# V for all heads ahead of the attention, tile 0 of the output projection scaled in the last head, and projection and gate_up in one block

## What is computed

```python
mod = silu(c) @ w_mod                      # six rows of 512: sa, ca, ga, sb, cb, gb
ga, gb = sign(g) * maximum(abs(g), 0.25)   # of both gates
h = layernorm(x) * (1 + ca) + sa
k, q, v = einsum(W_K, h), einsum(W_Q, h), einsum(W_V, h)       # per head
scores = q . k, below the diagonal (tril), others -1e10
attn = softmax(scores / sqrt(128));  z = attn @ v
x = x + ga * einsum('df,bqf->bqd', W_O, z_flat)
h = layernorm(x) * (1 + cb) + sb
gate, up = h @ dequant_fp4(gate_up)        # codes of 4 bits, scales per 128 inputs
y = (silu(gate) * up) @ dequant_fp4(down)
x = x + gb * y / sqrt(mean(y * y) + 1e-6)
```

## Time and profile before

| | us |
|---|---|
| median of the runs | 2183.33 |
| profiled execution | 2183.67 |
| its span, first to last instruction | 2181.7 |
| prologue | 0 to 57.4 |
| attention | 57.4 to 1664.7 |
| output projection | to 1877 |
| gate_up and down | to 2181.7 |

### The profile page before, as it was taken

One profiled execution on the slowest core, in us unless ns is written; L12 is line 12 of the kernel. 1 busy time (PEld: TensorE's weight loads), 2 busy tenths in 40 slices (PEclk: granted clock), 3 DMA queues, 4 the chain that ended last, 5 costly groups with the idle time before them and its releaser, 6 DMA issues. The chain is left out here.

```text
span 2181.7 us, 37262 instructions
## 1 busy us (share of the span) xinstructions
PE 2112.4 (97%) x12305; PEld 1845.1 (85%) x12305; DVE 1353.7 (62%) x3062; ACT 1059.6 (49%) x2006; POOL 719.3 (33%) x546
## 2 busy tenths in 40 slices
PE   6899999999999999999999999999997999899899
PEld 3698989898889989898988989898986788788687
DVE  7465655656565656556565646455564587699865
ACT  4354545455454545445454545455453333588511
POOL 3333343334243343443350101000017344388300
PEclk9999999999999999999999999999998999999999
DMA  5111110110111010111100000000006576111121
GB/s 207 40 41 35 35 34 32 35 43 22 46 46 34 34 34 31 34 34 34 46 25 26 25 12 24 12 22 15 25 21 192 175 245 221 57 40 39 46 70 63
DMA packets 84004, 122.79 MB, mean 56 GB/s; under 512 B 9315, under 2 KB 49891, under 8 KB 83939
## 3 DMA queue, kind: packets, MB, share of 16 engines
q1 hardware_dynamic: 81635, 117.76, 16.6%
q10 hardware_dynamic: 2304, 4.20, 0.5%
HBM read 87.97 MB, written 33.95 MB: 56 GB/s over the span
## 5 line engine op out<-in xcount | busy, mean ns | idle before, releaser
L978 DVE TENSOR_TENSOR pT_lo<-ps_t,pT_hi 128x512 fp32r<-128x512 f32 (+3 forms) x640 | 360.3, 605 | 219.9 <-ACT pT_hi L895 219.7
L903 ACT ACTIVATE probs<-probs,rmin 128x128 f32<-128x128 f32 (+15 forms) x256 | 307.9, 1203 | 225.7 <-DVE rmin L969 224.7
L895 ACT ACTIVATE pT_hi<-ps_t 128x512 fp32r<-128x512 f32 (+3 forms) x640 | 304.9, 534 | 87.5 <-PE ps_t L831 86.2
L197 PE MATMUL ps_z<-pT_hi,v_hi 128*128 128x256 f32 (+1 forms) x1152 | 326.4, 283 | 0.0
L198 PE MATMUL ps_z<-pT_lo,v_hi 128*128 128x256 f32 (+1 forms) x1152 | 325.4, 282 | 0.0
L199 PE MATMUL ps_z<-pT_hi,v_lo 128*128 128x256 f32 (+1 forms) x1152 | 324.8, 282 | 0.0
L197 PE MATMUL ps_p<-hT_hi,w_hi 128*128 128x512 f32 x768 | 309.6, 403 | 8.6 <-PEq L277 4.1
L199 PE MATMUL ps_p<-hT_hi,w_lo 128*128 128x512 f32 x768 | 301.9, 393 | 0.0
L198 PE MATMUL ps_p<-hT_lo,w_hi 128*128 128x512 f32 x768 | 301.2, 392 | 0.0
L831 PE MATMUL ps_t<-ident,probs 128*128 128x128 f32 x2176 | 278.9, 274 | 3.1 <-DVE pT_lo L978 1.6
L831 PEld LDWEIGHTS ps_t<-ident,probs 128*128 128x128 f32 x2176 | 247.3, 141 | 19.1 <-DVE pT_lo L978 2.1
(11 more groups left out here) (140 smaller groups left out, 3861.2 us busy)
## 6 DMA issues: line engine op xcount, KB each, us to landing
scratch_zT<-z SPq DMA_DIRECT2D x256, 64.0 KB, 1.6
o_z<-scratch_zT SPq DMA_DIRECT2D x31, 512.0 KB, 7.0
o_scales<-scratch_recips SPq DMA_DIRECT2D x31, 512.0 KB, 7.8
w_raw<-in_w_qkv SPq DMA_DIRECT2D x16, 768.0 KB, 4.6
p_wmod<-in_w_mod SPq DMA_DIRECT2D x6, 1024.0 KB, 10.6
words<-in_gu_packed SPq DMA_DIRECT2D x44, 128.0 KB, 3.5
scratch_wgu<-deq_a SPq DMA_DIRECT2D x22, 256.0 KB, 2.0
g_codes<-scratch_wgu SPq DMA_DIRECT2D x11, 512.0 KB, 3.4
```

The source lines that it names most:

```text
L197: nc.tensor.matmul(dst, stat[0], mov[0], start=start, stop=False)
L895: nc.scalar.activation(pT[0][:, slot, i % 2, 0:w], ps_t[:, (chunks_before(i) + u) % T_BANKS, 0:w], ACT.Copy).then_inc(t_hi, 1)
L903: nc.scalar.activation(probs[:, i % 2, 0:w], probs[:, i % 2, 0:w], ACT.Exp, bias=rmin[:, i % 2:i % 2 + 1], scale=-1.0, accum_out=sums[:, i ...
L978: nc.vector.tensor_tensor(pT[1][:, slot, i % 2, 0:w], ps_t[:, (chunks_before(i) + u) % T_BANKS, 0:w], pT[0][:, slot, i % 2, 0:w].bitcast(F ...
```

## The change

- **V pass.** The prologue computes V for all 16 heads, in 64 tiles of 128 tokens by four heads, with the tokens' hT as stationary operand, so that V needs no transposes. GpSimd (for the first group of heads, ScalarE with it) splits the V weights; ScalarE and VectorE split each tile of V, and SP saves both parts to a scratch tensor "v" in HBM, in two buffers. The prologue's steps are now in written orders too.
- **Attention.** The V and V^T units are gone, with their weights; SP loads both parts of V per head in four blocks of 512 tokens (load_v), the first two at the head's start. All three orders are new. Words, code, deq_a and deq_b lie in a buffer that belongs to tile 0 of the projection.
- **Last head.** SP loads z and reciprocals of tile 0, GpSimd scales all but head 15's part after the fourth part of W_O.
- **Output projection and gate_up** are one block: the projection returns its programs, and gate_up runs them first. The last tile's transposing and modulation stand among the first steps of gate_up. The gate scales are turned at tile 5 instead of 1. The first loads for down are issued behind the third load of gate codes.

The diff, cut to its core (in head of SP, attention):

```diff
 PE_ORDER = """
-    S0.0 S1.0 Z7.1- PW0 T0.0 T1.0 Z7.2- PK1.0 PK1.1 PK1.2 PK1.3 Z7.3- S2.0 N0- PQ1.0 PQ1.1 PQ1.2 PQ1.3 S3.0 Z0.0 T2.0
-    S4.0 S4.1 PV1.0 PV1.1 PV1.2 PV1.3 T3.0 T4.0 T4.1 S5.0 S5.1 PW1 Z1.0 S6.0 S6.1 S7.0 PK2.0 PK2.1 PK2.2 PK2.3 T5.0
-    T5.1 T6.0 S7.1 PQ2.0 PQ2.1 PQ2.2 PQ2.3 Z2.0 Z2.1 PV2.0 PV2.1 PV2.2 PV2.3 T6.1 T7.0 T7.1 PW2 S8.0 S8.1 S8.2 Z3.0
-    PK3.0 S9.0 S9.1 S9.2 PK3.1 Z3.1 PK3.2 PK3.3 T8.0 T8.1 T8.2 S10.0 S10.1 PQ3.0 PQ3.1 PQ3.2 PQ3.3 S10.2 T9.0 T9.1
-    T9.2 S11.0 S11.1 S11.2 Z4.0 T10.0 T10.1 T10.2 Z4.1 Z4.2 PV3.0 PV3.1 PV3.2 PV3.3 S12.0 S12.1 S12.2 S12.3 PW3 T11.0
-    T11.1 T11.2 S13.0 S13.1 S13.2 S13.3 Z5.0 T12.0 T12.1 Z5.1 Z5.2 T12.2 T12.3 T13.0 S14.0 S14.1 S14.2 PQ0.0+ PQ0.1+
-    S14.3 PQ0.2+ PQ0.3+ T13.1 T13.2 T13.3 S15.0 S15.1 S15.2 S15.3 Z6.0 Z6.1 Z6.2 T14.0 T14.1 T14.2 Z6.3 PK0.0+ PK0.1+
-    T14.3 T15.0 T15.1 PK0.2+ PK0.3+ T15.2 T15.3 Z7.0 PV0.0+ PV0.1+ PV0.2+ PV0.3+
+    S0.0 S1.0 S2.0 T15.0- T15.1- T15.2- PQ1.0 PQ1.1 PQ1.2 PQ1.3 Z7.0- Z7.1- T15.3- Z7.2- S3.0 Z7.3- N0- T0.0 T1.0
+    PK2.0 PK2.1 PK2.2 PK2.3 T2.0 S4.0 Z0.0 S4.1 PQ2.0 PQ2.1 PQ2.2 PQ2.3 T3.0 T4.0 T4.1 S5.0 S5.1 S6.0 Z1.0 PK3.0 S6.1
+    S7.0 S7.1 T5.0 T5.1 PK3.1 S8.0 S8.1 Z2.0 Z2.1 T6.0 T6.1 T7.0 S8.2 PK3.2 S9.0 T7.1 PK3.3 Z3.0 Z3.1 S9.1 S9.2 T8.0
+    T8.1 T8.2 S10.0 S10.1 PQ3.0 PQ3.1 PQ3.2 PQ3.3 S10.2 T9.0 T9.1 T9.2 S11.0 S11.1 S11.2 Z4.0 Z4.1 Z4.2 T10.0 T10.1
+    T10.2 S12.0 S12.1 S12.2 T11.0 T11.1 T11.2 PQ0.0+ S12.3 PQ0.1+ S13.0 Z5.0 Z5.1 Z5.2 S13.1 S13.2 S13.3 T12.0 T12.1
+    T12.2 S14.0 S14.1 T12.3 S14.2 PQ0.2+ PQ0.3+ S14.3 T13.0 T13.1 T13.2 S15.0 S15.1 PK0.0+ PK0.1+ PK0.2+ PK0.3+ Z6.0
+    Z6.1 T13.3 T14.0 T14.1 Z6.2 Z6.3 S15.2 S15.3 T14.2 T14.3 PK1.0+ PK1.1+ PK1.2+ PK1.3+
 """
...
 DVE_ORDER = """
-    C0.0 C1.0 X0 UW0 L0.0 L1.0 UK1 C2.0 UQ1 C3.0 L2.0 C4.0 C4.1 L3.0 L4.0 L4.1 C5.0 C5.1 UW1 C6.0 C6.1 X1 UK2 L5.0
-    L5.1 L6.0 C7.0 C7.1 UQ2 L6.1 L7.0 UW2 L7.1 C8.0 C8.1 C8.2 C9.0 C9.1 C9.2 X2 UK3 L8.0 L8.1 L8.2 C10.0 C10.1 C10.2
-    UQ3 L9.0 C11.0 C11.1 L9.1 L9.2 C11.2 L10.0 L10.1 L10.2 C12.0 C12.1 C12.2 C12.3 UW3 L11.0 C13.0 C13.1 C13.2 L11.1
-    L11.2 C13.3 L12.0 L12.1 L12.2 L12.3 L13.0 C14.0 C14.1 C14.2 C14.3 C15.0 L13.1 L13.2 L13.3 C15.1 C15.2 C15.3 UQ0+
-    R0 L14.0 L14.1 L14.2 L14.3 L15.0 L15.1 UK0+ L15.2 L15.3
+    C0.0 UK1 L15.0- L15.1- L15.2- UQ1 C1.0 L15.3- C2.0 X0 L0.0 L1.0 C3.0 UK2 L2.0 C4.0 C4.1 UQ2 L3.0 L4.0 L4.1 C5.0
+    C5.1 C6.0 X1 C6.1 C7.0 L5.0 L5.1 C7.1 C8.0 L6.0 L6.1 L7.0 C8.1 L7.1 C8.2 C9.0 X2 C9.1 C9.2 UK3 L8.0 L8.1 L8.2
+    C10.0 C10.1 C10.2 UQ3 L9.0 L9.1 L9.2 C11.0 C11.1 C11.2 L10.0 L10.1 L10.2 C12.0 C12.1 L11.0 L11.1 L11.2 C12.2 C12.3
+    C13.0 C13.1 C13.2 C13.3 L12.0 L12.1 L12.2 C14.0 C14.1 L12.3 C14.2 C14.3 UQ0+ L13.0 L13.1 L13.2 UK0+ C15.0 L13.3
+    L14.0 L14.1 C15.1 C15.2 C15.3 L14.2 L14.3 R0
 """
...
+UNITS = [("Q", 0), ("K", 0)] + [(kind, b) for b in range(1, NB) for kind in ("K", "Q")]
 UNIT_AT = {u: n for n, u in enumerate(UNITS)}
-SPLIT_UNITS = [u for u in UNITS if u[0] != "V"]
-SPLIT_AT = {u: n for n, u in enumerate(SPLIT_UNITS)}
-NU, NSU = len(UNITS), len(SPLIT_UNITS)
-MATS = ("Q", "K", "V")
...
+    PE_FIRST = """M0 M1 T0.0 T0.1 T0.2 T0.3 T1.0 T1.1 V0 V1 M2 T1.2 T1.3 V2 V3 T2.0 V4 T2.1 T2.2 T2.3 V5 V6 V7 V8 V9
+        V10 T3.0 T3.1 T3.2 V11 T3.3 M3 V12 V13 V14 M4 M5 V15"""
+    ACT_FIRST = """D0 H0 H1 H2 H3 A0.0 A0.1 A0.2 D1 A0.3 A1.0 A1.1 D2 Y0 Y1 D3 A1.2 A1.3 Y2 Y3 A2.0 Y4 A2.1 A2.2 A2.3
+        Y5 Y6 Y7 Y8 Y9 Y10 A3.0 A3.1 A3.2 Y11 A3.3 Y12 Y13 Y14 Y15"""
+    DVE_FIRST = """S0 G0 N0 G1 S1 L0.0 L0.1 L0.2 N1 L0.3 S2 S3 X0 L1.0 X1 G2 N2 X2 X3 L2.0 X4 N3 X5 X6 X7 X8 X9 X10 L3.0
+        X11 G3 X12 X13 X14 G4 G5 X15"""
+    POOL_FIRST = """I0 I1 I2 I3 WK WQ L1.1 J1.0 J1.1 L1.2 L1.3 J1.2 J1.3 L2.1 L2.2 L2.3 L3.1 L3.2 L3.3"""
+    SP_FIRST = """Rc Rm0 Rx0 Rm1 Rv0 Rx1 Rx2 Rx3 Rw Rm2 Rm3 Rv1 O0 O1 Rm4 O2 O3 O4 Rv2 O5 O6 O7 O8 O9 O10 O11 Rm5 O12
+        O13 O14 O15"""
+    V_FIRST = NT
...
+        def save_v(n):
+            g, t = divmod(n, NT)
+            sp.wait_ge(v_lo, n + 1)
+            for k in range(2):
+                sp.dma_start(hbm["v"][k, t, :, g * HG:(g + 1) * HG, :], vo[k][:, n % 2, :, :].bitcast(F32)) \
+                  .then_inc(v_saved[n % 2], 16)
+        for what, arg in entries(SP_FIRST):
+            if what == "R":
+                load(arg)
+            else:
+                save_v(int(arg))
+        for n in range(V_FIRST, NV):
+            if n == V_FIRST + 6:
+                load("v3")
+            save_v(n)
+        for n in range(2):
...
+        def wv_low(g, a):
+            pool.wait_ge(wv_hi, HG * g + a + 1)
+            nc.gpsimd.tensor_tensor(wv[1][:, g % 2, a, :], wv_raw[:, a, :], wv[0][:, g % 2, a, :].bitcast(F32),
+                                    ALU.subtract).then_inc(wv_lo, 1)
+
+        def wv_parts(g, a):
+            if a == 0:
+                pool.wait_ge(wv_loaded, 16 * (g + 1))
+                if g >= 2:
+                    pool.wait_ge(v_ready, NT * (g - 1))
+            nc.gpsimd.tensor_tensor(wv[0][:, g % 2, a, :], wv_raw[:, a, :], start.zeros[:, 0:1].to_broadcast([P, D]),
+                                    ALU.add).then_inc(wv_hi, 1)
+            wv_low(g, a)
+        for what, arg in entries(POOL_FIRST):
...
+        def value_hi(n):
+            act.wait_ge(v_ready, n + 1)
+            if n >= 2:
+                act.wait_ge(v_saved[n % 2], 2 * 16 * (n // 2))
+            nc.scalar.activation(vo[0][:, n % 2, :, :].rearrange("p h n -> p (h n)"), ps_v[:, n % 2, :], ACT.Copy) \
+              .then_inc(v_hi, 1)
...
+        def values(n):
+
+            g, t = divmod(n, NT)
+            if t == 0:
+                pe.wait_ge(wv_lo, HG * (g + 1))
+            if n >= 2:
+                pe.wait_ge(v_lo, n - 1)
+            dst = ps_v[:, n % 2, :].rearrange("p (h n) -> p h n", h=HG)
             for c in range(DC):
-                n = b * DC + c
-                if n >= 4:
-                    pe.wait_ge(h_ready, n - 3)
-                for t in range(TPB):
-                    last = nc.tensor.transpose(ps_t[:, n % 4, t * P:(t + 1) * P],
-                                               xn[:, t, c * P:(c + 1) * P], ident[:, :])
-                last.then_inc(t_ready, 1)
-            mod_section(b + 2)
+                if g == 0 and t % TPB == 0:
+                    wait_lo(pe, t // TPB, c)
+                ht = [part[:, c, t * P:(t + 1) * P] for part in (hT_hi, hT_lo)]
+                w = [part[:, g % 2, :, c * DH:(c + 1) * DH] for part in wv]
+                last = split_matmul(nc, dst, ht, w, c == 0, c == DC - 1)
+            last.then_inc(v_ready, 1)
...
+        def load_v(h, u):
+
+            if not is_at(h, 0):
+                if u < NB - 1:
+                    sp.wait_ge(z_read_v, (NB - 1) * (h - 1) + u + 1)
+                else:
+                    sp.wait_ge(z_ready, NPAIR * h)
+            for k in range(2):
+                sp.dma_start(v[k][:, u * TPB:(u + 1) * TPB, :].bitcast(F32),
+                             hbm["v"][k, u * TPB:(u + 1) * TPB, :, bass.ds(h, 1), :].rearrange("t p a n -> p t (a n)")) \
+                  .then_inc(v_loaded[u], 16)
...
         def head(h, decode, first, last):
+            for u in range(NB if first else 2):
+                load_v(h, u)
             if last:
-                sp.wait_ge(w_split, 6 * H)
+                sp.wait_ge(w_split, SPLITS * H)
                 for n in range(3):
                     load_wo(n)
             if not last:
-                sp.wait_ge(w_split, 6 * (h + 1))
-                sp.dma_start(w_raw[:, :, :], w_qkv[bass.ds(h + 1, 1), :, :, :].rearrange("a p m n -> (a p) m n")) \
+                sp.wait_ge(w_split, SPLITS * (h + 1))
+                sp.dma_start(w_raw[:, 0:2, :], w_qkv[bass.ds(h + 1, 1), :, 0:2, :].rearrange("a p m n -> (a p) m n")) \
                   .then_inc(w_loaded, 16)
             if decode:
                 load_piece(h, 0)
             if not first:
                 save_z(h - 1, NPAIR - 2)
+                for u in range(2, NB):
+                    load_v(h, u)
                 save_last_z(h - 1)
             if decode:
                 save_piece(h, 0)
...
+                sp.wait_ge(z_saved[0], Z_DMAS * 16 * (H * NPAIR // ZBUF - 1))
+                sp.dma_start(tile0.z[:, :, :], hbm["zT"][0]).then_inc(tile0.z_loaded, 16)
+                sp.wait_ge(recip_saved, 16 * (H - 1))
+                row = hbm["recips"][0:1, 0:H - 1, :].rearrange("a h n -> a (h n)")
+                sp.dma_start(tile0.scales[:, 0:H - 1, :].rearrange("p h n -> p (h n)"),
+                             row.to_broadcast([P, (H - 1) * P])).then_inc(tile0.scales_loaded, 16)
...
+        def scale_first_tile():
+            pool.wait_ge(tile0.z_loaded, 16)
+            pool.wait_ge(tile0.scales_loaded, 16)
+            for a, b in EARLY:
+                nc.gpsimd.tensor_tensor(tile0.z[:, a:b, :], tile0.z[:, a:b, :], tile0.scales[:, a:b, :], ALU.mult)
+
         def head(h, decode, last):
             if decode:
```

(28 more changed lines are left out.)

## The result

The changed kernel takes 2266.0 us (median of four runs, 2263.47 to 2269.09) against 2182.05 for the kernel before (median of four): a ratio of 1.0387, 95% interval 1.0363 to 1.0411. It is 84 us slower; 2252.7 was forecast. The profiled execution took 2263.7 us with a span of 2261.9, and it is read here against the 2181.7 of before.

The account below looks back on a forecast made before the run. An attention head was taken as bound by TensorE's own work. On 2183.67 us, 173.5 for the V pass, -199 for attention, +111 for the decode chain and -16.5 for seams gave +69: 2252.7 us, range 2200 to 2290.

Parts of the forecast that it names:

- V pass in the prologue: Prologue: computing V there makes attention begin at 231 us instead of 57.5, +173.5.
- V out of the heads: Attention: each head loses 12.6 us of V matmuls and transposes, leaving 86.9; with the last head's tail, -199 us.
- decode chain: Attention: unpackings wait for words; heads 1 to 10 take 9.9 us more each, head 0 about 12: +111 us.
- seams: Around the projection and gate_up: earlier loads, scaling and merged steps cut TensorE's idle time, together -16.5 us.
- bare tail: Last head: it ends with its own tile 15 and no projection to hide its long exponential, +2.5 us.
- rival 3: V pass: saves of V hold it back by 16 us or more, total 2269 to 2300; chance 0.09.
- V's loads and the words: Start of a decoding head: words queue behind v's loads and w_raw, landing at 13.2 to 15 us, taken as 14.2.
- the forecast's own loop: Decoding head: Z7.1 through words, X0, X1, X2 and S10.1 to the next Z7.1 takes 95.3 us instead of 86.9.
- The low end of the chain: Decoding heads: with words there when VectorE comes, the loop still adds 4.8 us a head.
- rival 2: Attention: v's loads hold no words back, only the chain X0, X1, X2 counts: 69 instead of 111, 2211 us; chance 0.1.
- The clock: Decoding heads: lower clock after TensorE's idle stretch behind X2 costs +1.5 us a head, bounds 0 and 3.
- Rival 1: Attention: VectorE's waits for words never reach TensorE, as VectorE can catch up in its idle time: 2142 us; chance 0.11.

Follow-up runs that it names:

- the kernel with all unpackings late: The kernel as changed, with X0, X1 and X2 all moved back in VectorE's order to later than their words can land: 2138.4 us.
- the saves doubled: Each save of V written a second time to a scratch place, on the kernel with all unpackings late: 2226.1 us.
- The experiment with w_raw: The kernel as changed, with the words of piece 0 issued ahead of w_raw but still behind the two loads of v: 2245.2 us.
- where X1 and X2 no longer wait: The kernel as changed, with X1 moved ahead of C9.1 and X2 behind C12.1, X0 left in place: 2180.9 us.
- the undone seam: The kernel with all unpackings late, with tile 0's loads put back behind the last saves and its scaling behind the splitting of wo: 2151.4 us.
- a third buffer: Three buffers instead of two for V's tiles on their way out, on the kernel with the saves doubled: 2167.5 us.

## Why the forecast came out as it did

The ledger of the profiled executions. What V's leaving gave is read from the kernel with all unpackings late, whose attention lasted 1401.5 us, and the chain's price is the rest:

| term | forecast | measured |
|---|---|---|
| V pass in the prologue | +173.5 | +182.8 |
| V out of the heads | -199 | -205.8 |
| decode chain | +111 | +123.6 |
| seams | -16.5 | -20.4 |
| sum | +69 | +80.2 |

The mechanism was right: loop, places, who waits for whom, and the sign. That the kernel came 13 us above the forecast is due to two terms that were sized too low and two, smaller, that were too cautious.

**V leaves the heads.** 86.9 us a head was forecast and 86.8 measured, in the four heads without decoding and in all heads once the unpackings stood late. The 2.5 us for a bare tail were wrong in sign: 16 x 12.7 = 203.2 went, and 2.6 more beside. The tail does wait 2.7 us for its last exponential; most of what went beside lies in the last head: from the turn before its own to its own it takes 90.8 us in the kernel before and 79.4 in the kernel with all unpackings late, 11.5 less, where three of its four units of V are worth 9.5. Why, the runs do not show.

**The V pass.** 64 tiles 2.74 us apart, as forecast; rival 3 did not come about. The saves land 2.6 and 3.3 us behind their issue (median of the high and the low part), longer than the 2.0 taken, and just within the 3.3 worked out as free; ScalarE waits for them 20 times, TensorE once, for 0.9 us. The Trainium skill's page "DMA: Bandwidth & Descriptors" (Latency and other measured facts), weighed in the prediction, would have made it an estimated 3.8 under high load; at 182 GB/s the trace shows less than that, and at 250, with the saves doubled, 4.5 and 5.2. What failed is the step "the first tile of V needs block 0 of hT_lo, 28.1": it took the time from the kernel before, whose orders are others. The wait of 10.5 us for tile_z in the list above is T1 behind N1, and V0 stood behind T1: 31.4, which is +3.3. The work behind it had a mean granted clock of 0.97 (199.3 us busy instead of 195.3), +4.0, and 9.5 us were idle instead of 8.

**V's loads and the words.** "13.2 to 15, I take 14.2" was the step that mattered most: the words landed at 16.4 in the head. The rate had been worked out as 330 GB/s, from one landing in an otherwise quiet head, and the bytes behind the words were left out: two parts of z and two more blocks of v go out while the words are still under way, and the engines deliver 277 GB/s to all of them. One save of z, issued at 748.05 behind the words, even landed ahead of them (751.98 against 752.41). By the two stretches above, 2.27 MB moved between 743.0 and 752.4, 0.43 more than the 1.84 that were counted: at 277 GB/s an estimated 1.6 of the 2.2 us. The experiment with w_raw shows what 0.5 MB ahead of the words costs, 1.9 us of X0's start in the mean. By the forecast's own loop, 53.7 + 8.1 + 16.3 + 16.3 + 1.6 + 0.9 + 0.7 = 97.6, and the undisturbed heads have 97.6. The round trips hold to 0.2 us, and so does the sum of the rest.

**The low end of the chain.** The range had put a head with its words in time at +4.8, and rival 2 at 2211. Measured 95.5 in the mean and 2229.8. The step was "VectorE reaches X0 at 10.6 (behind L15.3 and C2.0)": it left out that C2.0 waits for T0.0. The true floor is 13.2.

**The clock.** +1.5 a head was taken, bounds 0 and 3; the mean of the ten heads lies 1.0 above the undisturbed ones. About 0.6 of it lies between S10.1 and the next Z7.1, where the granted clock is low in the disturbed heads (0.79 from 590 to 598 us in one of them, 1.00 from 788 to 796 in an undisturbed one); most of the rest is words that land later, up to 1.2 us, which is not the clock's. In a head of 100.2 us of the kernel after, two stretches at X0's wait of 3.6 us and one behind that for X2, where the granted clock is between its two levels of 2.4 (1.00) and 1.2 GHz (0.50):

```profile
1047.00:1052.00 5.00, 1.97 (x9) 1.98 (x10) 4.28 (x11) 1.13 (x3) 2.42 (x3) 0.70 0.56 143
1052.00:1057.00 5.00, 5.00 (x17) 3.99 (x18) 0.44 (x5) 1.18 (x4) 4.84 (x4) 0.61 0.00 0
...
1082.00:1087.00 5.00, 4.29 (x11) 2.95 (x12) 4.56 (x13) 1.45 (x2) 0.00 (x0) 0.66 0.00 0
```

What is lost behind X0 is taken back in the next wait, as the prediction said of X1: in this head TensorE waits 1.1 us behind X1 instead of 2.4. **Head 0** cost 6.5 us, not 12 (attention's start to the first turn of the reciprocals takes 113.5 us against 107.0 with the unpackings late): with no Z7 its words come in time, and 12 had simply been too much.

**A third wait was missing.** The prediction had TensorE idle before S8.0 and S10.1. It is idle before Z0.0 too, since L0.0 and L1.0 stand behind X0. In the loop this adds nothing, and the forecast time didn't need it; but where X1 and X2 no longer wait it is the wait that counts. That kernel came 15 us above its expectation, which had the wait at its size and the slow clock behind it at nothing.

**Seams.** -7 was forecast for the start of the projection and -7.0 measured (4.3 us of waiting instead of 11.3); the undone seam gives the same edit a price of 11 to 13, since there the scaling comes on top of the load. The second wait of the earlier trace rows, 3.1 us, is gone, and between projection and gate_up TensorE waits 0.4 and 1.6 us.

**Rival 1** held 0.11 and was the sign's hinge. It was wrong for this order and is nearly the time of the same change with three entries moved: 2142 against 2138.4.

## What to carry to other kernels

Where one buffer makes a round trip (load, unpack, decode on another engine, save, load again), measure the trip and keep its steps at least that far apart in every in-order list; speeding up the work around them moves them closer together without a line about them being changed. Where several waits lie on one loop, removing one of them moves its time to the next or makes it worse: find the loop's length first, then stretch the distances or shorten the trip. Before a new placement is priced, list what each neighbour in the list itself waits for; the place of a step is the latest of these, not its rank.

## What was not expected of the hardware

**VectorE and GpSimd hold each other up, and by chance.** VectorE's four tensor_scalar of block 0 (L600) took 1.91, 2.87, 3.88 and 4.83 us in four of these kernels whose prologues are the same up to there, when they began at 14.24, 14.41, 14.65 and 15.12; GpSimd's first subtraction on the V weights began at 15.4 to 15.7. Most that fall beside one of GpSimd's take about the length of that one. Between two of them a start 0.4 us later thus cost 2 us more, and attention began at 235.5 in one profiled execution and at 240.6 in another with the same prologue. The pattern is finer than these four: in another kernel the same four began at 14.20 and took 2.97 us, since the last of them began just beside GpSimd's first subtraction (15.58 and 15.62). The Trainium skill's page "SBUF — State Buffer" (SBUF: two separate sides) describes such a pair of ports, shared by the two engines and held by one for the whole of an instruction while the other is fully blocked; the traces here agree, with 0.48 us an instruction alone and 1.26 beside.

**A full share of the DMA engines is no rate.** 0.99 went with 245 GB/s and two buffers, 1.03 with 312 GB/s and three, and 1.03 again with 360 GB/s in the next 50 us, for the same transfers. The Trainium skill's page "Perfetto Trace Analysis" (Identifying the Most-Contended Engine) warns of the same, that the occupancy of 16 DMA engines misleads. Here it would have led to blaming the rate for 59 us that a third buffer gave back.
